# A recurrent kernel's second load of W_ih over two DMA queues, and its weight sums in four pieces on VectorE

## What is computed

```python
def cell(h, x):
    gi = x @ W_ih + b_ih
    gh = h @ W_hh + b_hh
    i_r, i_z, i_n = jnp.split(gi, 3, axis=-1)
    h_r, h_z, h_n = jnp.split(gh, 3, axis=-1)
    r = jax.nn.sigmoid(i_r + h_r)
    z = jax.nn.sigmoid(i_z + h_z)
    n = jnp.tanh(i_n + r * h_n)
    h_new = (1.0 - z) * n + z * h
    return (h_new, h_new)
x = x + _L0_cond_ref(x, cond_2048[:, None, :], L0_cond_b)
x = x + _L1_cond_ref(cond_2048, x, L1_cond_W_ih, L1_cond_W_hh, L1_cond_b_ih, L1_cond_b_hh)
```

## Time and profile before

| what | value |
|---|---|
| median of three runs | 1174.54 us (1171.37 to 1176.35) |
| the profiled execution | 1172.44 us |
| its span, first to last instruction | 1170.6 us |
| TensorE busy | 1116.4 us, 95% of the span, 5254 matmuls |
| VectorE busy | 797.3 us, 68% |
| ScalarE busy | 535.8 us, 46% |
| GpSimd busy | 441.1 us, 38% |
| mean granted TensorE clock | 0.991 of full speed |

### The profile page before, as it was taken

How to read it: one execution, slowest core, us unless ns; L and a number is a source line. 1 busy time by engine, 2 the same in 40 slices (tenths; PEclk the granted TensorE clock), 3 DMA queues, 4 the chain that set the end, 5 groups by cost and what they waited for, 6 DMA issues and landing times.

```text
span 1170.6 us, 15057 instructions
## 1 busy us (share of the span) xinstructions
PE 1116.4 (95%) x5254; PEld 933.0 (80%) x5254; DVE 797.3 (68%) x1231; ACT 535.8 (46%) x1012; POOL 441.1 (38%) x734
## 2 busy tenths in 40 slices
PE   1999999999999599999999999999999999999996
PEld 1977888888888487888888888888888888888885
DVE  2746676676774646677777777777777777777774
ACT  3536776777774153243443333343344333344332
POOL 0352112122012724344455554444455554444332
PEclk9999999999999889999999999999999999999999
DMA  9999899888845401011111111111111111111101
GB/s 249 280 233 190 183 195 191 187 191 194 189 122 122 102 21 35 18 37 36 37 36 36 37 34 30 30 35 36 37 37 36 37 34 30 30 34 37 28 19 27
DMA packets 233228, 101.65 MB, mean 87 GB/s; under 512 B 212944, under 2 KB 217552, under 8 KB 231104
## 3 DMA queue, kind: packets, MB, share of 16 engines
q1 hardware_dynamic: 212544, 66.11, 25.8%
q0 software_dynamic: 16256, 33.32, 10.4%
q10 hardware_dynamic: 4352, 1.25, 0.4%
HBM read 66.49 MB, written 34.14 MB: 86 GB/s over the span
## 4 chain that ended last, share of the span: by engine, by line
PE 91%; DMA 3%; DVE 3%; ACT 1%; issue 1%; ACTq 1%; SPq 0%; POOL 0%; DVEq 0%; POOLq 0%
PE bank L1095 55%; PE bank L1142 26%; PE bank L1117 5%; PE bank L1057 2%; PE bank L1084 2%; DMA w_again<-in_L_cond_W_ih_dram 1%; DVE comb L902 1%; DMA early<-early_result 1%; ACT toep_early L665 0%; DMA xres<-stage 0%; DMA tap_pad<-tap_rows 0%; SPq L480 0%; ACTq L641 0%; DVE comb_lo L929 0%; DMA xT<-early 0%
## 5 line engine op out<-in xcount | busy, mean ns | idle before, releaser
L1095 PE MATMUL bank<-w_hh_hi,hT_hi 128*128 128x512 f32 x768 | 299.7, 390 | 0.1
L1095 PE MATMUL bank<-w_hh_lo,hT_hi 128*128 128x512 f32 x768 | 299.4, 390 | 0.0
L1095 PE MATMUL bank<-w_hh_hi,hT_lo 128*128 128x512 f32 x768 | 298.8, 389 | 0.0
L532 POOL DMA_DIRECT2D out_dram<-outZ x256 | 139.1, 550 | 248.5 <-DVE outZ L1040 246.3
L1095 PEld LDWEIGHTS bank<-w_hh_hi,hT_lo 128*128 128x128 f32 x768 | 144.2, 188 | 30.6
L1095 PEld LDWEIGHTS bank<-w_hh_hi,hT_hi 128*128 128x128 f32 x768 | 144.4, 188 | 28.5 <-issue 0.5
L1095 PEld LDWEIGHTS bank<-w_hh_lo,hT_hi 128*128 128x128 f32 x768 | 144.4, 188 | 27.6
L775 ACT ACTIVATE r<-bank 128x512 f32<-128x512 f32 x64 | 38.3, 598 | 205.6 <-PE bank L1095 204.8
L785 ACT ACTIVATE n_gate<-q 128x512 f32<-128x512 f32 x64 | 40.5, 634 | 197.9 <-DVE q L986 197.9
L525 POOL DMA_DIRECT2D xT<-xres x192 | 104.7, 550 | 19.6 <-issue 13.0
L1095 PE MATMUL bank<-w_ih_hi,xT_hi 128*128 128x512 f32 x240 | 97.1, 405 | 14.8 <-ACT bank L684 14.8
(11 more groups left out here) (140 smaller groups left out, 2193.8 us busy)
## 6 DMA issues: line engine op xcount, KB each, us to landing
x_unit<-in_x_dram SPq DMA_DIRECT2D x64, 256.0 KB, 5.1
toep_ring<-kernel_parts SPq DMA_DIRECT2D x128, 128.0 KB, 3.6
out_dram<-outZ POOLq DMA_DIRECT2D x256, 64.0 KB, 2.0
xres<-stage SPq DMA_DIRECT2D x32, 384.0 KB, 5.0
xT<-xres POOLq DMA_DIRECT2D x192, 64.0 KB, 2.1
early<-early_result SPq DMA_DIRECT2D x4, 1024.0 KB, 13.6
xT<-early POOLq DMA_DIRECT2D x60, 64.0 KB, 3.3
w_ih_raw<-in_L_cond_W_ih_dram SPq DMA_DIRECT2D x12, 256.0 KB, 7.5
```

The costliest lines, as they stand in the source:

```text
L532: pool.dma_start(out[:, t, :].rearrange("(Q s) (q e) -> q s Q e", s=QUAD, e=P)[q4], outZ[t % 2][q4 * QUAD:(q4 + 1) * QUAD, :].rearrange("s ...
L1095: mm = nc.tensor.matmul(psum[:, :], a[:, rows], b[w][:, cols], start=False, stop=stop and n == 2, skip_group_check=True)
```

## The change

- SyncE and ScalarE each issue two DMAs of W_ih, one for a quarter of the partitions with all three gates in it (`w_again_quarter`). SyncE's come behind its last stores, without a wait for their landing; ScalarE's come at the end of step 13. Both wait until the convolution's matmuls (`conv_done`) and its low parts (`x_lo_ready`) are done. `w_again` moves to the place of the buffers `x_unit` and `toep_ring`, and `comb_hi` takes its place, so no high part may be written before all sums are made.
- GpSimd makes no sums. VectorE makes all 21, in four pieces: five behind `xT_lo` and five behind the new h in step 15, five and six at the same places in step 16.
- The high parts: two at the end of step 16, two, three and three in step 17, two in step 18. The low parts: two behind `xT_lo`, two behind the second operation on `q` and three behind the new h in step 17, three behind `xT_lo` in step 18, two at the start of step 19.
- TensorE waits for one low part at the first use of each combined product. `COMBINED` is put in the order of use; `COMBINED_AT` keeps the places in SBUF.
- In `load_xT` at step 13 a loop is written otherwise and issues the same DMAs in the same order.

```diff
-COMBINED = (14, 6, 11, 17, 7, 16, 9, 20, 5, 8, 10, 15)
+COMBINED = (14, 6, 17, 11, 9, 20, 16, 7, 5, 8, 15, 10)
+COMBINED_AT = (14, 6, 9, 11, 17, 20, 16, 7, 5, 8, 15, 10)
...
-        COMB_DVE = 12
+        COMB_DVE = 21
...
+        def w_again_quarter(q4):
+            return (w_again[q4 * QUAD:(q4 + 1) * QUAD, :].rearrange("r (k n) -> r k n", k=KB),
+                    w_ih[q4 * P:(q4 + 1) * P, :].rearrange("(k r) n -> r k n", r=QUAD))
...
             sp.wait_ge(conv_done, NBANK)
-            for n in range(2):
-                sp.wait_ge(stage_stored[n], 32 * (PAIRS // STAGE // 2))
-            for g in GATES[0]:
-                for q4 in range(QUADS):
-                    sp.dma_start(
-                        w_again[q4 * QUAD:(q4 + 1) * QUAD, :].rearrange("r (k n) -> r k n", k=KB)[:, :, g:g + D],
-                        w_ih[q4 * P:(q4 + 1) * P, g:g + D].rearrange("(k r) n -> r k n", r=QUAD),
-                    ).then_inc(w_again_loaded, 16)
+            sp.wait_ge(x_lo_ready, NBLOCK)
+            for q4 in range(QUADS // 2):
+                sp.dma_start(*w_again_quarter(q4)).then_inc(w_again_loaded, 16)
...
-                if t == EARLY - 1:
-                    combine_weights()
                 pool.wait_ge(outZ_ready, t + 1)
...
+                if t == BULK_LAST:
+                    act.wait_ge(conv_done, NBANK)
+                    act.wait_ge(x_lo_ready, NBLOCK)
+                    for q4 in range(QUADS // 2, QUADS):
+                        act.dma_start(*w_again_quarter(q4)).then_inc(w_again_act_loaded, 16)
...
+            def combine_first():
+                dve.wait_ge(w_again_loaded, 16 * QUADS // 2)
+                dve.wait_ge(w_again_act_loaded, 16 * QUADS // 2)
                 put(14, k_block(0, "z"), k_block(0, "n"), ALU.subtract)
...
+                put(8, k_block(0, "n"), k_block(0, "z"), ALU.subtract)
+                put(14, so_far(14, 1), k_block(1, "n"), ALU.add)
+                put(6, so_far(8, 2), k_block(1, "n"), ALU.subtract)
+                put(14, so_far(14, 3), k_block(1, "r"), ALU.subtract)
...
                 if t == EARLY - 1:
-                    combine_weights()
+                    combine_first()
+                if t == EARLY:
+                    combine_third()
+                if t == EARLY + 1:
+                    low_combined(0, 2)
+                if t == EARLY + 2:
+                    low_combined(7, 3)
+                if t == EARLY + 3:
+                    low_combined(10, 2)
...
+                if t == EARLY - 1:
+                    combine_second()
+                if t == EARLY:
+                    combine_fourth()
+                if t == EARLY + 1:
+                    low_combined(4, 3)
...
             def x_product(l, psum, start=False, stop=True):
+                if l not in multiplied:
+                    multiplied.add(l)
+                    if l in COMBINED:
+                        pe.wait_ge(comb_lo_ready, COMBINED.index(l) + 1)
...
-                        pe.wait_ge(comb_lo_ready, len(COMBINED))
```

More of the change, by code:

```diff
@@ L167, in conv_residual_gru @@
     top[0] = x_at
-    comb_hi = place("comb_hi", len(COMBINED) * D, F32R)
     comb_at = top[0]
@@ L174, in conv_residual_gru @@
     w_again = place("w_again", KB * NG)
-    comb_u, comb_e = place("comb_u", D), place("comb_e", D)
-    assert top[0] <= conv_end
     top[0] = comb_end
+    comb_hi = place("comb_hi", len(COMBINED) * D, F32R)
     SIZES = {"F": 7, "G": 8, "H": 4}
@@ L290, in conv_residual_gru @@
         assert BULK_LAST < EARLY and (BULK_LAST - BULK_FIRST + 1) * POINTS >= NBANK
-        assert FIRST % 2 == 0 and FIRST >= EARLY + 4
+        assert FIRST % 2 == 0 and FIRST >= EARLY + 2
         def last(t):
@@ L326, in comb_cols @@
         def comb_cols(product):
-            at = COMBINED.index(product) * D
+            at = COMBINED_AT.index(product) * D
             return slice(at, at + D)
@@ L535, in store_out @@
                     ).then_inc(out_stored[t % 2], 16)
[L537 to L563, removed]
             def sum_x(t, group):
@@ L609, in step @@
                         pool.wait_ge(stage_stored[n], 32 * (PAIRS // STAGE // 2))
-                    for late in range(EARLY, t + RING + 1):
+                    for late in range(EARLY, t + RING):
                         load_xT(late)
-                if t > BULK_LAST and t + RING < T:
+                if t >= BULK_LAST and t + RING < T:
                     load_xT(t + RING)
@@ L778, in step @@
                     put_gate(t + 1, "r")
-                if t == EARLY:
-                    high_combined(0, 4)
+                if t == EARLY + 1:
+                    high_combined(2, 2)
+                if t == EARLY + 2:
+                    high_combined(10, 2)
                 first_half(bulk_bank(t, 1))
@@ new lines, in combine_second, with combine_third @@
+            def combine_second():
+                put(15, k_block(1, "r"), k_block(1, "z"), ALU.subtract)
+                put(10, k_block(3, "z"), k_block(3, "n"), ALU.subtract)
+                put(14, so_far(14, 5), k_block(2, "r"), ALU.subtract)
+                put(16, so_far(15, 6), k_block(2, "r"), ALU.add)
+                put(7, k_block(2, "n"), so_far(10, 7), ALU.subtract)
+            def combine_third():
+                put(20, k_block(0, "r"), k_block(0, "z"), ALU.subtract)
+                put(17, so_far(16, 9), k_block(2, "z"), ALU.subtract)
+                put(8, so_far(8, 2), k_block(2, "n"), ALU.add)
+                put(9, so_far(20, 11), k_block(3, "r"), ALU.subtract)
+                put(17, so_far(17, 12), so_far(7, 10), ALU.add)
@@ new lines, in combine_fourth @@
+            def combine_fourth():
+                put(5, so_far(20, 11), k_block(2, "r"), ALU.add)
+                put(11, so_far(9, 14), k_block(0, "n"), ALU.add)
+                put(20, so_far(9, 16), k_block(2, "n"), ALU.add)
+                put(11, k_block(1, "n"), so_far(11, 17), ALU.subtract)
+                put(20, so_far(20, 18), k_block(3, "n"), ALU.add)
+                nc.vector.tensor_scalar(so_far(20, 20), so_far(20, 20), -1.0, None,
+                                        ALU.mult).then_inc(comb_dve_ready, 1)
```

50 lines of the change are left out of this document (15 added, 35 removed).

## The result

The changed kernel takes **1154.59 us** (median of 4 runs, 1152.78 to 1155.91) against 1172.95 us for the kernel before, run beside it (median of 4, 1166.82 to 1176.35). The ratio is 0.9844, with a 95% interval of 0.9809 to 0.9878; the medians differ by 18.4 us. The profiled execution took 1152.78 us, its span is 1150.9 us and its mean granted clock 0.998. The span before was 1170.6 us: 19.7 us are gone, where the working said 19.8.

The account below looks back on a forecast made before the run. TensorE, busy 95%, bounds the kernel, so only its waits and low clock can be won: 17.0 plus 2.7, 19.8 us before rounding. From 1172.44 that gives 1152.7, from the old median 1154.8; forecast 1154 us, range 1151 to 1160.

Parts of the forecast that it names:

- the load: W_ih for step 15: 4.2 MB at 231 GB/s, bytes the limit, landing at 386 us, at the late end 389.8.
- What bounds the kernel: TensorE waiting or at low clock: step 15 loses 17.0 us, step 18 2.7, priced against 16.80 us per neighbouring step.
- the edit of the queue: Second queue for W_ih: by the skill's rule no rate, landing nearer 389.8 us, gain 19.3 instead of 19.8 us.
- The margin: Step 15: `q` may start at 392.9 us, so W_ih may land at 389.3 us without cost.
- The 21 sums: VectorE's four pieces, steps 15 and 16, at 0.72 us per sum fit its idle time: cost nothing; uncovered, 3.6 to 5.0 each.
- GpSimd gone: Step 15: VectorE's 6.93 us subtraction, beside GpSimd on the same buffers, falls to 0.72; inside the 14.1 us, not counted again.
- The splits and waits: Step 18: three low parts take 3.0 us, `q` fits with nothing over; TensorE's waits per product cost nothing.
- A: Rival: x of step 16 lands late, at 390.4 to 394.2 us, costing 2.4 to 6.2 us: 1156 to 1160 us; chance 0.18.
- B: Rival: VectorE and GpSimd hold each other up in steps 17 to 19: 1155 to 1156 us; chance 0.10.
- C: Rival: W_ih lands far too late for step 15; above 1180.4 us if behind 412.5 us; chance 0.02.
- D: Rival: the old waits stay because something else holds `q`; half of step 15's loss staying gives 1162.5 us; chance 0.03.

## Why the prediction was right

The forecast was 1154 us and the median is 1154.59. The cleaner comparison is with the profiled executions, 1172.44 and 1152.78 us: 19.7 us, where the sum has 19.8. One term of the reasoning, the load, was wrong and did no harm, which was luck.

**What bounds the kernel.** TensorE's standing still and its low clock in two places: right. The cadence of `hT_hi` priced both whole, 17.0 and 2.7 us, and 17.03 and 2.74 came. This step carried the prediction: the price of a loss was read off neighbouring steps that do the same work without it, so no estimate of why VectorE was slow had to be right.

**The load.** The landing was forecast at 386 us and came at 384.7, but the reasoning was wrong and the near hit is luck. I took the 231 GB/s of the earlier trace rows, at a share of 1.04, for the limit of the engines. It was the rate of one queue that loads quarters of the partitions, with GpSimd's loads beside it. At about the same share the changed kernel's queues together went to 387 GB/s, and the row of 55 to 60 us in the kernel before had 426. ScalarE's half was in at 366.4 + 10.2 = 376.6 us, SyncE's moved behind the stores, at 200 to 212 GB/s from 378 to 382 us, and from the first issue to the last landing it took 384.7 - 366.0 = 18.7 us, close to my 18 plus one. The Trainium skill (DMA: Bandwidth & Descriptors, Rules for kernel authors) advises against splitting over partition halves and says that more queues save issue time only. The runs here differ: with one queue W_ih landed at 391.8 us, with two at 384.7, and the measurement decides that splitting this load was worth it; whether the queues or the partitions did it stays open. By my own argument the edit of the queue was worth 0.5 us, and by the run it is worth 1.5, of which `xT`, held up as well, is a part.

**The margin.** `q` may start 11.0 us behind step 14's `hT_hi`, read from the rows of before, came out the same in five experiments (`q` less TensorE's wait, with one queue, with the late and the old load, with one piece and with GpSimd held back). With it, a landing after 389.3 us was said to cost; at 391.65 us the old load cost 1.3 us of the cadence, of which 1.0 was a wait.

**The 21 sums.** In a row each takes 0.60 us and not 0.72, which is the pitch of sums that each wait for the one just before: 3.0 us for a piece of five instead of 3.6. The multiplication took 0.43 us (at 415.72), inside its bounds of 0 and 1.4, and `hT_lo` still had 0.85 us of idle time ahead of it. Cost at nothing was right, and the experiment with one piece shows what the cover hides: 7.5 us.

**GpSimd gone.** The 6.93 us row was right to be called a collision and to be left inside the 14.1 us. By the run it and its neighbours were 8.4 us of the step.

**The splits and waits.** The three low parts of step 18 took 3.52 us, 1.17 each against the 1.01 I used. `q` still waited 0.48 us for TensorE, so what I had called a fit with nothing over had 0.5 us over: `xT_lo` and the first accumulation took 441.57 - 436.89 - 3.52 = 1.2 us, where I had put 2.

**The rivals.** A (a late `xT`) showed its mechanism at 385.79 us, where ScalarE idled for `xT` [2.43] and not for TensorE as before, but it was two microseconds inside what is free. In the one-queue kernel it cost 1.2 us of waiting. B (mutual hold-ups later) shows as the 1.17 us of the low parts and cost nothing. C and D left no trace.

How the 19.7 us divide depends on what is already in place. From the kernel before, the collision alone is 8.4 us; from the changed kernel, going back to one piece costs 7.5, to the old sums 8.0 in step 15 and 2.0 in step 16, to the old load 1.3, and to one wait for all low parts at the old place 5.6. They overlap and don't add up to 19.7: each opens the same wait again.

## What to carry to other kernels

Price a stall by the cadence of equal steps before asking for its cause: this gives the gain whole, low clock included, and the cause only has to be removed. Work of VectorE that has no deadline of its own belongs in pieces into the idle time ahead of operations that wait for others, and TensorE should wait for the one piece that it uses next. Full shares of the DMA engines do not mean full rate: look for the highest rate that the same trace shows at a full share, and at which queues and partitions carry the packets, before calling bytes the limit.

## What the runs showed of the hardware that I had not expected

- A share of 1.0 of the DMA engines went with very different rates: 200 to 212 GB/s for W_ih on one queue in DMAs over 32 partitions, 272 for it on two queues to different partitions, 387 with W_ih, stores and GpSimd's DMAs on three queues, and 426 for one queue alone that stores from all 128 partitions. How much of this is the queues and how much the partitions, the direction or the size of the DMAs was not separated.
- A two-input operation on VectorE can be shut out across several of GpSimd's: 5.98 us for one of 0.69. In the kernel before with GpSimd held back the same operations, also beside GpSimd's sums, took 1.16 to 1.66 us. What decides between the two I did not settle.
- The granted clock fell to 0.50 (1.2 GHz) behind a wait of 3.7 us, and that cost 1.9 us more. Behind the 2.5 us wait of before it was at 1.00, and step 18 lost 2.7 us in all. Waits of 5.7, 6.4, 7.6 and 14.1 us cost 1.8, 2.2, 2.2 and 2.9 us in low clock: most of the price comes with a wait of 3.7 us, and it then grows far more slowly than the wait.
- What an issue costs the issuing engine is not fixed: on ScalarE 0.32 and 0.46 us for two DMAs, and 1.33 us for each of five more behind a first, so that it stood still for 6.47 us; on SyncE 5.06 us for the four of W_ih right behind its stores, and 1.99 us for the same four when issued late into an idle queue. This looks like the price of a queue that is full; no run tested that by itself.
